# Counting a graph's edges in one-hot products: 64 slots for each destination node instead of 128 for a pair

## The reference

```
h = relu(layernorm(x))
for l in range(3):
    mlp = lambda z: relu(z @ W1[l] + b1[l]) @ W2[l] + b2[l]
    msgs = mlp(h[dst])                      # edge_index = [src, dst]; row, col = src, dst
    agg  = segment_sum(msgs, src, N)
    h    = mlp(h + agg)
out = x + h @ Wf + bf
```

## Time and profile before

| what | value |
| --- | --- |
| time, median of 3 runs | 2164.39 us (2163.72 to 2164.8) |
| profiled execution, its own time | 2161.14 us |
| its span | 2159.4 us |
| busy: PE, DVE, ACT, POOL | 2025.7, 1454.3, 793.6, 609.3 us |
| groups of the build | 196, of them 164 with a fused unit |

### The profile page before, as it was taken

One profiled execution on the slowest core, in us unless ns is written; L12 is line 12 of the kernel. 1 busy time (PEld: TensorE's weight loads), 2 busy tenths in 40 slices (PEclk: granted clock), 3 DMA queues, 4 the chain that ended last, 5 costly groups with the idle time before them and its releaser, 6 DMA issues.

```text
span 2159.4 us, 39820 instructions
## 1 busy us (share of the span) xinstructions
PE 2025.7 (94%) x15741; PEld 1138.4 (53%) x15741; DVE 1454.3 (67%) x1656; ACT 793.6 (37%) x2228; POOL 609.3 (28%) x273
## 2 busy tenths in 40 slices
PE   4565889999999999999999999999999999999998
PEld 3444445555565555555555555555555555555554
DVE  7999999999999999946643343343365444434433
ACT  4996887777777778722200000000010000000000
POOL 3666666666767666600000000000000000000000
PEclk8796999999999999999999999999999999999999
DMA  7356666666666666653444543543543555555452
GB/s 201 75 137 186 178 170 207 189 200 197 193 194 193 189 191 188 190 175 90 150 149 120 164 146 107 164 149 111 172 149 113 179 160 154 159 159 159 142 164 71
DMA packets 332829, 344.51 MB, mean 160 GB/s; under 512 B 21562, under 2 KB 303992, under 8 KB 332184
## 3 DMA queue, kind: packets, MB, share of 16 engines
q1 hardware_dynamic: 327516, 335.59, 52.6%
q0 software_dynamic: 2352, 6.43, 1.1%
q10 hardware_dynamic: 2816, 0.53, 0.2%
HBM read 252.58 MB, written 89.89 MB: 159 GB/s over the span
## 4 chain that ended last, share of the span: by engine, by line
PE 75%; DVE 15%; issue 3%; DMA 3%; ACT 2%; POOL 1%; SPq 1%; DVEq 0%; POOLq 0%; ACTq 0%
PE ps L1525 48%; PE ps L1404 15%; DVE arena L754 7%; PE ps L1375 4%; PE ps L1399 4%; DVE arena L762 3%; DMA arena<-counts_dram 2%; PE ps L1481 2%; PE ps L1503 1%; POOL arena L636 1%; PE ps L1487 1%; DVE arena L802 1%; SPq L453 1%; DVE arena L794 1%; ACT arena L1182 1%
## 5 line engine op out<-in xcount | busy, mean ns | idle before, releaser
L1525 PE MATMUL ps<-arena,parts 128*128 128x448 fp8e4 x5488 | 1049.1, 353 | 0.8 <-DVE arena L890 0.8
L1525 PEld LDWEIGHTS ps<-arena,parts 128*128 128x128 f16 x5488 | 534.7, 98 | 514.2 <-issue 24.6
L636 POOL TENSOR_TENSOR arena<-arena,weight_now 128x416 int32<-128x416 int32 x196 | 518.3, 2644 | 273.6 <-DVE arena L754 271.3
L877 DVE TENSOR_SCALAR arena<-arena 128x3136 uint16<-128x3136 uint16 x196 | 191.4, 976 | 592.2 <-PE ps L1525 592.2
L1404 PE MATMUL ps<-arena,parts 128*128 128x448 fp8e4 x2744 | 550.8, 353 | 1.5 <-DVE parts L843 1.5
L754 DVE TENSOR_TENSOR arena<-row_iota,key_now 128x3840 f16<-128x3840 f16 (+1 forms) x196 | 425.8, 2172 | 0.0
L1404 PEld LDWEIGHTS ps<-arena,parts 128*128 128x128 f16 x2744 | 266.4, 98 | 291.2 <-issue 73.1
L1274 ACT ACTIVATE arena<-arena 128x448 f32<-128x448 f32 x42 | 24.2, 577 | 988.9 <-DVE arena L904 988.9
L1182 ACT ACTIVATE arena<-ps 128x800 uint16<-128x800 f32 x392 | 338.4, 872 | 31.4 <-PE ps L1375 31.0
L1375 PE MATMUL ps<-arena 128*128 128x53 fp8e4 x6272 | 205.3, 189 | 76.6 <-POOL arena L636 64.1
L1375 PEld LDWEIGHTS ps<-arena 128*128 128x128 f16 x6272 | 195.6, 98 | 125.3 <-DVE arena L754 76.7
(11 more groups left out here) (150 smaller groups left out, 1176.7 us busy)
## 6 DMA issues: line engine op xcount, KB each, us to landing
arena<-counts_dram SPq DMA_DIRECT2D x294, 784.0 KB, 4.6
counts_dram<-arena SPq DMA_DIRECT2D x784, 100.0 KB, 2.2
h_dram<-parts SPq DMA_DIRECT2D x2, 1536.0 KB, 7.2
edges_dram<-arena SPq DMA_DIRECT2D x2, 1400.0 KB
arena<-in_x_dram SPq DMA_DIRECT2D x14, 192.0 KB
out_dram<-arena SPq DMA_DIRECT2D x14, 192.0 KB
arena<-in_dst_dram SPq DMA_DIRECT2D x1, 1400.0 KB
arena<-in_src_dram SPq DMA_DIRECT2D x1, 1400.0 KB
```

The lines of the kernel that those rows point to most:

```text
L636: nc.gpsimd.tensor_tensor(pairs, pairs, weight_now[:, h * HW:(h + 1) * HW].unsqueeze(2).to_broadcast([P, HW, WORDS // 2]), ALU.mult).then_ ...
L877: v.tensor_scalar(spread[:, c % WIDE, 0, :].bitcast(U16), packed, 0x0F0F, None, ALU.bitwise_and)
L1525: last = t.matmul(ps[:, b, 0:NB], parts[:, c * CK + k, :], spread[:, c % WIDE, b // 2, at:at + NB].bitcast(F8), start=start, stop=stop)
```

## The change

- **Slots.** Each dst node, not each pair, gets 64 slots (REACH). Slots 0 to 63 hold edges of a pair's first node and 64 to 127 those of its second, so a window takes two indirect DMAs, each at its own start.
- **Rows.** A row one-hot is 64 wide (ROWS) for each slot instead of 128. `row_iota` holds numbers 64 higher on partitions 64 to 127. ScalarE's part in the rows (FEW, `few_far`, `few_now`) goes.
- **Products.** Each of the 32 products becomes two, 64 slots x 64 rows by 51 columns, on the quarter (partitions 0 to 63 to output rows 0 to 63) and the quarter (64 to 127 to 64 to 127). The moving operand is f16 instead of fp8.
- **Columns and weights.** The column one-hots (`hot_m`) are 50 halfwords plus one; `weigh` multiplies 32 x 25 = 800 32-bit words. The weight is a whole f16; the passes that made `e2` go. The columns' numbering changes accordingly (`word_iota`, WORD_BASE).
- **Starts.** Units hold 8 edges (GRAN), so 408 rises per product (FANX), exact as a high and a low f16 part, two matmuls each. The last edge of a unit is used, with the first 64 edges of the next partition loaded too (`dst_next`). Starts are found for both nodes (two Sign passes). 20 windows (BATCHES x BATCH) get theirs in the prologue, the other 29 one by one in windows j = 13 to 41 of the build (`node_step`, `make_fan_now`, `count_fan_now`, `find_starts`).
- `ADDED` is empty, so `add_sums` is never issued; `sums_freed` gives the same waits as before in another form.

The core of the diff:

```diff
-GRAN = 16
+GRAN = 8
+REACH = WIN // 2
+BATCH = 4
+BATCHES = 5
+FAN_AHEAD = 7
-WORDS = 2 * 13
+WORDS = 2 * LP
-COLS = 2 * WORDS + 1
+COLS = WORDS + 1
+ADDED = ()
...
-                pool.indirect_dma_start(win[:, t % WR, :], None, edges_dram.rearrange("(r f) -> r f", f=2 * GRAN),
-                                        bass.IndirectOffsetOnAxis(ap=start_i[:, t:t + 1], axis=0)).then_inc(
-                    windows_gathered[t % WR], 16)
+                for d in range(2):
+                    pool.indirect_dma_start(win[:, t % WR, d * WIN:(d + 1) * WIN], None,
+                                            edges_dram.rearrange("(r f) -> r f", f=2 * GRAN),
+                                            bass.IndirectOffsetOnAxis(ap=start_i[:, t, d:d + 1], axis=0)).then_inc(
+                        windows_gathered[t % WR], 16)
...
-                pairs = hot_c[:, k % SLOTS, :, 0:WORDS].bitcast(I32)
+                pairs = hot_m[:, k % SLOTS, :, 0:WORDS].bitcast(I32)
...
+            def node_step(t):
+                if t > FANS:
+                    dve.wait_ge(s["fans_made"], BATCHES + t - FANS)
+                v.tensor_scalar(step_now, node_pairs, float(2 * P * pair_at(t)), tops, ALU.add, ALU.is_ge).then_inc(
+                    s["steps_made"], 1)
...
-                link(v.tensor_scalar(e2[:, c], src_t[:, c], 4, None, ALU.bitwise_and), dve)
-                link(v.tensor_scalar(e2[:, c].bitcast(F32), e2[:, c], 32.0 * 255 / 4, 32.0, ALU.mult, ALU.add), dve)
...
-                v.scalar_tensor_tensor(pk_weight[:, units, :], by_units(e1)[:, units, :], 0.25,
-                                       by_units(e2.bitcast(F32))[:, units, :], ALU.add, ALU.mult).then_inc(s["edges_packed"], 1)
+                v.tensor_scalar(pk_weight[:, units, :], by_units(e1)[:, units, :], 4096.0, 15360.0, ALU.mult,
+                                ALU.add).then_inc(s["edges_packed"], 1)
...
-                few = FEW if k >= FEW_FROM else 0
-                compare_keys(hot_r[:, slot, few:HW, :].rearrange("p c (m two) -> p c m two", two=2), row_iota[:], P,
-                             key_now[:, u, 0, w.start + few:w.stop, :]).then_inc(s["rows_made"], 1)
+                compare_keys(hot_r[:, slot, :, :].rearrange("p c (m two) -> p c m two", two=2), row_iota[:], ROWS,
+                             key_now[:, u, 0, w, :]).then_inc(s["rows_made"], 1)
...
+                if fan_of(j) >= 0 and h == 0:
+                    node_step(fan_of(j))
+                if fan_of(j) >= 0 and h == 3:
+                    find_starts(fan_of(j), 1)
...
+            def count_fan(t, frm, scrap):
+                for d in range(2):
+                    a.activation(scrap[:, d, :], frm[:, 0:FANX], ACT.Sign, scale=-1.0, bias=node_less[:, d, t:t + 1],
+                                 accum_out=signs[:, t, d:d + 1])
...
+            def make_fan(to, steps):
+                for part in range(2):
+                    last = t.matmul(to, steps, rises[:, part, 0:FANX + 1], start=part == 0, stop=part == 1)
+                return last
...
-                        last = t.matmul(product(q)[:, c, 0:COLS], hot_r[:, slot, w, :], hot_c8[:, slot, w, 0:COLS], start=True,
-                                        stop=True)
+                        for d in (slice(0, REACH), slice(REACH, WIN)):
+                            last = t.matmul(product(q)[d, c, 0:COLS], hot_r[d, slot, w, :], hot_m[d, slot, w, 0:COLS],
+                                            start=True, stop=True)
```

More of the change, by code:

```diff
@@ L386, in unit_of, with sums_freed @@
             return j - AHEAD if j >= AHEAD else -1
+        def sums_freed(u, b):
+            if u >= SB and b in ADDED:
+                return s["sums_added"], len(ADDED) * (u - SB) + ADDED.index(b) + 1
+            left = [n for n in range(SBB) if n not in ADDED]
+            if u >= SB:
+                return s["sums_kept"], SBB * SB + len(left) * (u - SB) + left.index(b) + 1
+            return s["sums_kept"], SBB * u + b + 1
         def chunks_before(g):
@@ L691, in _ @@
-            node_steps(0)
-            dve.wait_ge(s["firsts_shifted"], 1)
-            v.tensor_tensor(rises[:, 0:FAN], firsts, ps[0:EP, 0, 0:FAN], ALU.subtract).then_inc(s["rises_made"], 1)
-            for n in range(1, GROUPS):
+            v.tensor_copy(lasts[:, 0:FAN], by_units(dst_t)[:, :, GRAN - 1])
+            v.tensor_scalar(lasts[:, FANX:FANX + 1], dst_t[:, EC - 1:EC], 1.0, None, ALU.add)
+            dve.wait_ge(s["next_loaded"], 16)
+            v.tensor_copy(lasts[:, FAN:FANX], by_units(dst_next)[:, :, GRAN - 1]).then_inc(s["lasts_made"], 1)
@@ L695, in _ @@
+            for n in range(BATCHES):
                 node_steps(n)
@@ L722, in _ @@
+            for n in range(2):
+                find_starts(n * BATCH, BATCH)
             less, var, inv, tmp = (stat[:, j, :] for j in range(4))
@@ L728, in _ @@
                 if t.start == 0:
-                    for n in range(3, 5):
-                        find_starts(n)
+                    for n in range(2, 4):
+                        find_starts(n * BATCH, BATCH)
             link(last, dve)
@@ L738, in _ @@
             v.tensor_tensor(less, counted[:, 1, 0, :], counted[:, 1, 1, :], ALU.add)
-            for n in range(5, GROUPS):
-                find_starts(n)
+            for n in range(4, BATCHES):
+                find_starts(n * BATCH, BATCH)
             dve.wait_ge(s["root_made"], 1)
@@ L976, in _ @@
                     turn_counts(k - LAG)
+                before = unit_of((k - 1) // HG)
+                if before >= SB and (k - 1) % HG in ADDED:
+                    add_sums(before, (k - 1) % HG, (k - 1) % 2)
                 if h == 0 and u >= 0:
@@ L1264, in _ @@
                     keep_weights()
-            keep_sums(FUSED - 1, SBB - 1, (SBB - 1) % 2)
-            for b in range(SBB):
-                keep_sums(FUSED, b, b)
+            for u, b in [(FUSED - 1, SBB - 1)] + [(FUSED, b) for b in range(SBB)]:
+                if b not in ADDED:
+                    keep_sums(u, b, b if u == FUSED else b % 2)
             def epilogue(l, i):
@@ L1462, in _ @@
                     turn_keys(j + 1)
+                if h == 1 and fan_of(j) >= 0:
+                    make_fan_now(fan_of(j))
                 if unit_of(j) >= 0:
```

269 lines of the change are left out of this document (152 added, 117 removed).

## The result

The changed kernel takes 2223.84 us (median of 4 runs, 2221.65 to 2226.91); the kernel before takes 2164.6 in the same runs. The ratio is 1.0272, 95% interval 1.0254 to 1.029: slower by 59 us, where 45 were forecast. The profiled execution took 2221.65 us, its span is 2219.6.

A forecast was written before the change was run, and what follows sets the result against it. VectorE and TensorE were taken to tie at 4.36 us per fused group. Terms: 16 (weigh) + 16 (gather) + 25 (starts) - 6 - 6 (ahead of fusion) = +45 us, giving 2209 us; range 2137 to 2305.

The forecast's parts named there:

- The mechanism named for it: Fused groups: GpSimd and VectorE taking turns at their shared port set the pace, 4.70 us per group; chance 0.44.
- rival 1: Fused groups: TensorE becomes the bound, its products keeping 26 ns spacing; 5.26 us per group, 2301 us in all; chance 0.22.
- The tie before: Fused groups, kernel before: TensorE and VectorE both without gaps at 4.36 us per group; gaining on one alone is worth nothing.
- The compares: VectorE, per fused group: rows fall from 2.07 to 1.14 us, columns rise from 0.51 to 0.91; together 0.53 saved.
- weigh: GpSimd's multiply, per fused group: 1.48 us for 0.77, stalling VectorE's unpack 0.62 us; net +0.10 x 164 = +16 us.
- gather: GpSimd's queue: two indirect DMAs per window delay one multiply in four groups; 0.10 us per group taken, +16 us.
- Who sets the pace: Fused groups: VectorE and GpSimd at 4.70 us per group, TensorE just under at 4.58.
- I take 1.0: TensorE, per fused group: the 64 products on quarters take 1.0 us, where the 32 before took 0.84.
- Starts: VectorE in the build: node_step and find_starts in 29 windows, 0.85 us each, +25 us; 0 if that side has slack.
- Ahead of the fused part: Before the first fused unit: packing the edges gives -6 us, the 32 groups ahead of fusion another -6.
- All groups counted alike: Fused groups: the per-group differences were multiplied by all 164 groups with a fused unit.
- Behind the build: After 922 us: the change leaves these stretches alone and they keep their length; no term in the sum.

## Why the prediction was right, and where not

The direction and the range held (2223.84 within 2137 to 2305, +59 us for +45). The mechanism named for it was only the second of the two. The sign put down for rival 1, 64 products over 1.1 us with TensorE gapless, is the one that came.

- **The tie before.** Right as far as the runs go: making one side dearer in the kernel before costs in full, 52 us on TensorE's and 90 on the port's. That relieving one alone there is worth nothing was not run. Both sides became dearer, TensorE's by more.
- **The compares.** 1.13 and 0.90 us from start to start for 1.14 and 0.91 forecast.
- **weigh.** A tail of 1.40 us for 1.48; the unpack is held up by 0.46 us for 0.62. VectorE's plain group is 4.27 us for 4.45.
- **gather.** One late multiply per window, as forecast: the unpack takes 1.0 us more once in four groups (0.25 per group, 0.10 forecast). It costs nothing while TensorE sets the pace.
- **Who sets the pace.** This step failed. "I take 1.0" for the 64 products was too low: they take 1.12, and the next instruction 0.11 more. TensorE's group is 4.72, 4.83 with a fan, and not 4.58. I had put the point from which TensorE decides at 1.1 us, and it was passed. That the quarters work beside each other was right; what the 1.0 had too low are the spacing of the pairs (31.7 ns for 26, 0.20 us per group) and the price of changing shape (0.20). The first rival has the right engine and the wrong price: 64 products at 26 ns each, 1.68 us, where 1.12 + 0.11 were measured, 0.45 less. The run with quarters alone gives +52 us for the change's +59, so the loss is TensorE's. VectorE's side is right behind it, at 4.70 in the run on the whole array against 4.70 in the forecast; that the sum came out is partly luck, smaller stalls against dearer gathers and waits for starts.
- **Starts.** 25 us were charged, on VectorE. The run with the starts ahead shows 6 us in groups 52 to 168, and by the chain the fan costs TensorE 0.29 us in each of 27 windows, 8 us; VectorE's part costs nothing while TensorE sets the pace.
- **Ahead of the fused part.** -12 us were forecast, -0.4 measured at group 32. The packing did shrink, by 5.3 us (13.7 for 19.0; 5 to 6 forecast). But it began 2.1 us later, at 21.09 us, when `src` had landed, and the last store took 9.0 us (35.16 to 44.14) for about 6.8. So the first gather starts at 44.5 us for 45.5. Then twelve gathers of 1.25 us stand in a row ahead of the first multiply, which I had not costed on POOL's queue: the multiply starts 2.7 us later (61.1 for 58.4) although its row compare starts 1.3 earlier. By TensorE's products group 0 comes 1.4 us later and the 32 groups gain 1.8, where 6 were forecast. This term is 12 us of the 15 by which the forecast is short.
- **All groups counted alike.** The forecast multiplied by 164. Twenty-eight of them (32 to 59) have no kept sums on TensorE, and up to 313 us VectorE has one more pass in every second group, 0.60 us from start to start (L843): 4.74 us before. There the change gains 1.4 us. The other 136 lose 0.43 each and not 0.35. That 164 x 0.35 = 57 us and the measured 56.6 from group 32 to 195 are so near is luck.
- **Behind the build.** 4.4 us behind the last instruction weren't forecast; the stretches keep their length, as forecast.

The sum again, by the products' starts: -0.4 up to group 32 (-12 forecast), 56.6 in the fused groups (57), -0.4 + 4.4 behind them (0): 60.2 us.

## What to carry to other kernels

Where two engines tie, price a change on both, and put the larger uncertainty on the one that the trace shows without any gap: 0.1 us there was worth 14 us here, in the 136 groups where TensorE has no gap. Small products on two quarters are best issued in turn (1.12 against 1.83 us for 64). Even then a pair that replaces one whole product gained nothing here, and each change of shape had a price of its own. And a longer GpSimd instruction costs VectorE nothing until it outlasts what VectorE can run without the shared port: here one transpose of 0.93 us.

## What the runs showed of the hardware

- Products of 64x64 by 51, at a granted clock of 1.00: on two diagonal quarters in turn, a pair starts every 31.7 ns, its two products 3 to 4 ns apart; on one quarter alone a product starts every 31 to 32 ns. Products on the whole array start every 26 ns. With what comes behind them, 64 take 1.12 us in turn (17.5 ns each) and 1.83 us in runs of 16 on one quarter (28.6); 32 whole ones take 0.83. So splitting a 128x128 product into two diagonal quarters costs a third more and saves nothing.
- Going from whole-array chunk matmuls to products on quarters took 0.09 us more than going to whole products, and going back 0.11 more; the chain shows the latter in the next instruction, whether a transpose or an f32 matmul.
- GpSimd's int32 multiply takes 0.74 to 0.77 us for 416 and 1.40 us for 800 elements behind the instruction that blocks it, 0.90 and 1.55 us when the port is free.
- Indirect DMAs in a row on GpSimd's queue start 1.25 us apart. The second one per window added 4.4 us between the last computing instruction and the end of the span.
